# A transformer layer on one core: a new beginning, both first halves first, and the causal mask of four groups added by VectorE

## The reference, cut to what matters

```python
x = x + attention(layernorm(x))          # x: 2 sequences x 1024 tokens x 128
x = x + moe(layernorm(x))

def attention(x):                        # 16 heads of 8, causal
    q, k, v = x @ Wq.T, x @ Wk.T, x @ Wv.T         # per head
    q, k = rope(layernorm_head(q)), rope(layernorm_head(k))
    s = where(tril, q @ k.T / sqrt(8), -inf)
    return (softmax(s) @ v) @ Wo.T + bo

def moe(x):                              # 16 experts of 64, 2 per token, one shared of 128
    p = softmax(x @ gate_w.T)            # best 2 of 4 groups of experts, then best 2 experts
    y = sum_e combine[:, e] * (silu(x @ We1 + be1) * (x @ We3 + be3) @ We2 + be2)
    return y + silu(x @ ws1 + bs1) * (x @ ws3 + bs3) @ ws2 + bs2
```

## Time and profile before

| | |
|---|---|
| median of 3 runs | 455.01 us (453.49 to 484.75) |
| the profiled execution | 456.76 us, of it a span of 454.9 us from the first to the last instruction |
| busy share of the span | PE 84%, DVE 68%, ACT 59%, POOL 44% |
| mean granted TensorE clock | 0.910 |

### The profile page before, as it was taken

One profiled execution on the slowest core, in us unless ns is written; L12 is line 12 of the kernel. 1 busy time (PEld: TensorE's weight loads), 2 busy tenths in 40 slices (PEclk: granted clock), 3 DMA queues, 4 the chain that ended last, 5 costly groups with the idle time before them and its releaser, 6 DMA issues.

```text
span 454.9 us, 6876 instructions
## 1 busy us (share of the span) xinstructions
PE 382.1 (84%) x2295; PEld 138.7 (30%) x2295; DVE 309.4 (68%) x622; ACT 269.6 (59%) x395; POOL 198.7 (44%) x294
## 2 busy tenths in 40 slices
PE   3542898779599898999997999998988999979786
PEld 2221233132133242223243332222423322434332
DVE  4676978795827897558355899757878761439543
ACT  2524048337659844185877943684585799865460
POOL 1304966964693424144141454632222332268441
PEclk9865659868979998699999999999999999997899
DMA  6966023000400035000050044000000001540271
GB/s 146 181 116 138 1 57 86 0 2 1 118 22 4 1 79 110 1 1 2 1 141 3 1 98 90 2 1 0 3 0 2 1 3 46 112 78 0 55 134 46
DMA packets 26036, 21.48 MB, mean 47 GB/s; under 512 B 8817, under 2 KB 21778, under 8 KB 25938
## 3 DMA queue, kind: packets, MB, share of 16 engines
q1 hardware_dynamic: 24610, 19.99, 20.3%
q10 hardware_dynamic: 1392, 1.05, 1.1%
HBM read 13.43 MB, written 1.18 MB: 32 GB/s over the span
## 4 chain that ended last, share of the span: by engine, by line
PE 48%; DVE 16%; ACT 10%; DMA 8%; issue 7%; POOL 7%; SPq 2%; ACTq 1%; POOLq 0%; DVEq 0%
PE psum L809 11%; PE psum L791 7%; PE psum L844 6%; PE psum L855 6%; PE psum L767 6%; DMA comb_b<-combine_scratch 5%; DVE mx_full L1199 5%; ACT probs L917 4%; PE psum L732 3%; PE psum L761 3%; DVE mx_diag L1199 3%; PE psum L741 1%; ACT sq L934 1%; PE psum L859 1%; DMA xs<-in_x 1%
## 5 line engine op out<-in xcount | busy, mean ns | idle before, releaser
L917 ACT ACTIVATE probs<-psum 128x1024 f32<-128x1024 f32 x144 | 140.6, 1027 | 24.1 <-PE psum L791 21.7
L1199 DVE TENSOR_REDUCE mx_diag<-psum 128x4 f32<-128x512 f32 (+2 forms) x96 | 97.3, 1041 | 41.2 <-PE psum L767 40.8
L1199 DVE TENSOR_REDUCE mx_full<-psum 128x2 f32<-128x1024 f32 x64 | 75.8, 1218 | 24.3 <-PE psum L767 24.1
L1111 POOL TENSOR_SCALAR_AFFINE_SELECT probs<-probs 128x256 f32<-128x256 f32 (+1 forms) x112 | 47.6, 442 | 90.4 <-ACT probs L917 87.9
L809 PE MATMUL psum<-probs,v_ones 128*9 128x512 f32 (+3 forms) x768 | 79.8, 505 | 6.9 <-POOL probs L1111 6.6
L844 PE MATMUL psum<-x2T,w 128*128 128x512 f32 x144 | 77.1, 639 | 5.8 <-ACT mv L954 2.7
L1121 POOL TENSOR_TENSOR mh<-mh,mv 128x512 f32<-128x512 f32 x36 | 45.6, 1270 | 76.6 <-DVE mv L1271 76.6
L767 PE MATMUL psum<-k_st,q_st 62*128 62x512 bf16 (+3 forms) x384 | 61.7, 356 | 3.1 <-DVE mx_full L1199 2.9
L791 PE MATMUL psum<-q_st,k_st 64*128 64x512 bf16 (+3 forms) x384 | 54.3, 333 | 8.7 <-ACT probs L917 6.4
L855 PE MATMUL psum<-mh,w 128*128 128x512 f32 x72 | 42.6, 693 | 6.0 <-POOL mh L610 3.4
L1271 DVE SCALAR_TENSOR_TENSOR mv<-psum,b,mv 128x512 f32<-128x512 f32 x36 | 26.4, 745 | 23.6 <-ACT mh L966 23.5
(11 more groups left out here) (150 smaller groups left out, 393.3 us busy)
## 6 DMA issues: line engine op xcount, KB each, us to landing
comb_b<-combine_scratch SPq DMA_DIRECT2D x8, 1024.0 KB, 10.0
q_st<-parts SPq DMA_DIRECT2D x24, 128.0 KB, 2.5
k_st<-parts SPq DMA_DIRECT2D x18, 128.0 KB, 2.5
w<-in_We SPq DMA_DIRECT2D x3, 512.0 KB
k_st<-in_c_pad SPq DMA_DIRECT2D x2, 512.0 KB, 8.1
out<-xs SPq DMA_DIRECT2D x4, 256.0 KB, 2.3
xs<-in_x SPq DMA_DIRECT2D x3, 256.0 KB, 10.2
k_st<-parts ACTq DMA_DIRECT2D x6, 128.0 KB, 4.1
```

What stands on the lines that cost most here:

```text
L917: act.activation(probs[:, n % P_RING, :, :], wpair("scores", (s, i)), ACT.Exp, scale=SCALE).then_inc(exp_done, 1)
L1111: last = pool.affine_select(out=v, in_=v, compare_op=ALU.is_ge, fill=0.0, base=0, pattern=[[0, v.shape[1]], [1, P]], channel_multiplier=-1)
L1199: dve.tensor_reduce(dst[:, a % 2, qt, :, pairs[0]:pairs[0] + nm], w, AX.X, ALU.max, negate=True).then_inc(max_free, 1)
```

## The change

1. **Order of the chunks.** Chunk x becomes half `x // 2` of sequence `x % 2`: both first halves, then both second halves.
2. **The layernorm before attention is folded away.** The raw x is transposed. The weights are centred by one more product (`wcenter`: with I - 1/128). q and k need no factor of the token, since each head is normalised again (the epsilon is scaled by the token's variance: `eps_x`); v is multiplied by the token's reciprocal root as ACT copies it (`values`). `norm` splits into `stats` and `norm`; `norm_apply` and `xn` go.
3. **Chunk 0's preparation is cut by tiles** and spread over ACT (`square`), DVE (`products`, `headsum0`, straight from PSUM), POOL (`join`); the factor of the head comes last (`rope_q`, then `rope_k`, so that `qT` starts before k is ready). Its lowest part of k is made by DVE.
4. **The reciprocal roots** take 8 operations on DVE (a Newton step, then a step of higher order), not 10; on POOL 12 of other kinds, not 15. The stages of POOL are cut finer (seven for a chunk).
5. **Loads.** Inputs are packed on the host; SP issues 10 loads, not 39. `w_attn` is issued by ACT behind chunk 0's x. The padding rows are set by memsets: `q_st` by DVE, `k_st` by POOL, each half of `k_st` on its own. `stack` waits for each of the three parts by itself.
6. **`mneg` of groups 0 to 3** is done by DVE (`mneg_dve`).
7. **Groups 4 to 7** (now the first half of sequence 1): no mask matmuls. DVE adds the mask and takes the maximum in one `tensor_tensor_reduce` for each head's rows.
8. **The planner** has other lengths, windows and `PV_LAG`, and `NUDGES`, which shift the urgency of single stages.

The diff, cut to its core (the numbers of `NUDGES`, the packing on the host and renamings are left out):

```diff
+def seq_of(x):
+    return x % B
+def half_of(x):
+    return x // B
+def keys_of(x):
+    return [y for y in range(x + 1) if seq_of(y) == seq_of(x)]
...
-PREP_WINDOWS = ((-282.3, -241.5), (-192.9, -118.6), (269.8, 447.0), (500.9, 602.6))
-EPILOGUE_WINDOWS = ((-268.0, -266.3), (-631.0, -532.6), (262.1, 401.0), (76.9, 130.6))
-MOE_WINDOWS = ((52.4, 357.9), (166.5, 310.2), (303.6, 553.6), (401.9, 560.1))
-PV_LAG = 152.8
+PREP_WINDOWS = ((-728.2, -501.8), (-276.2, -260.9), (325.2, 359.2), (740.3, 741.2))
+EPILOGUE_WINDOWS = ((-259.4, -227.3), (-714.1, -661.4), (253.0, 450.8), (-388.2, 27.1))
+MOE_WINDOWS = ((52.1, 369.6), (329.2, 365.2), (381.8, 511.7), (442.6, 536.5))
+PV_LAG = 126.2
+SPLIT_ON_DVE = NG
+MASKED_BY_DVE = range(4,8)
+ROPE_OF = ((),) + (("rstd_seed", "rstd_step", "rope_scale", "rope_cos", "rope_sin", "rope_add", "rope_join"),) * 3
...
+            if part == 0:
+                if which == 0 and x >= 2:
+                    engine.wait_ge(work_full, turned(*LAST_SCORES[NG * (x - 1) - 1]))
+                elif which == 0:
+                    engine.wait_ge(q_blank, 1)
+                else:
+                    engine.wait_ge(k_blank, b + 1)
+                engine.wait_ge(part_hi, 2 * x + which + 1)
+            elif part == 1:
+                engine.wait_ge(part_mid, 2 * x + which + 1)
+            elif (x, which) == (0, 1):
+                engine.wait_ge(first_low, 1)
+            else:
+                engine.wait_ge(parts_lo, 2 * x + which + (x == 0))
+            for t in [t for t, p in enumerate(terms) if p == part]:
+                engine.dma_start(dst[t::HD], parts[:, which, part, :]).then_inc(done, 16)
...
+            sp.dma_start(mats[:, :, :], c_mats).then_inc(ld_attn, 16)
+            sp.dma_start(rowb[:, :], vectors.partition_broadcast(P)).then_inc(ld_tabs, 16)
+            sp.dma_start(tabs[:, :], c_tabs).then_inc(ld_tabs, 16)
+            sp.dma_start(xs[:, 1, :, :], x_v[1]).then_inc(ld_x[1], 16)
+            sp.dma_start(gate_raw, gate_w).then_inc(ld_gate, 16)
+            sp.dma_start(experts[:, :], w_moe).then_inc(ld_moe, 16)
+            sp.dma_start(b2[:, :], b_moe).then_inc(ld_moe, 16)
...
+            def whole():
+                w = fill("wcenter", 0)
+                pe.wait_ge(work_read_act, frees("act", turned("weights", 0)))
+                pe.matmul(w[:, 0:3 * P], whole_mean, w_whole, start=True, stop=True).then_inc(work_full, 1)
...
+                masked_here = what == "diag" and a not in MASKED_BY_DVE
+                if masked_here:
                     for par in range(2):
                         v = w[:, par, 0:nm * keys].rearrange("p (m k) -> p m k", m=nm)[:, :, keys - P:keys]
                         pe.matmul(v, ident_bf[:, :], causal_bf[:, :].unsqueeze(1).broadcast_to([P, nm, P]),
...
             act.dma_start(xs[:, 0, :, :], x_v[0]).then_inc(ld_x[0], 16)
+            act.dma_start(w_raw[:, :, :], w_attn).then_inc(ld_attn, 16)
...
+            def first_products(t):
+                dve.wait_ge(squared, t + 1)
+                both = wbank("qkv0", t)[:, 0:2 * P]
+                cos = g_cos[:, 0, t, :, :, :].rearrange("p w r d -> p (w r d)")
+                dve.tensor_tensor(first_cos[:, t, :, :], both.rearrange("p (n m) -> p n m", m=H // 2),
+                                  cos.unsqueeze(2).broadcast_to([P, 4 * HD, H // 2]), ALU.mult)
...
+            def first_rope(w):
+                dve.wait_ge(joined, TPC)
+                r = hrstd[:, :].rearrange("p (t n m) -> p t n m", t=TPC, m=H // 2)
+                for par in range(2):
+                    s = roped[:, :, w, par, :, :]
+                    last = dve.tensor_tensor(s, s, r[:, :, 2 * w + par, :].unsqueeze(2).broadcast_to(
+                        [P, TPC, HD, H // 2]), ALU.mult)
+                link(last)
+                for par in range(2):
+                    s = roped[:, :, w, par, :, :]
+                    last = dve.tensor_tensor(s, s, g_add[:, 0, :, w, par, :].unsqueeze(3).broadcast_to(
+                        [P, TPC, HD, H // 2]), ALU.add)
+                last.then_inc(first_roped, 1)
...
-                dve.tensor_reduce(dst[:, a % 2, qt, :, pairs[0]:pairs[0] + nm], w, AX.X, ALU.max, negate=True).then_inc(max_free, 1)
+                if what == "full" or a not in MASKED_BY_DVE:
+                    last = dve.tensor_reduce(dst[:, a % 2, qt, :, pairs[0]:pairs[0] + nm], w, AX.X, ALU.max, negate=True)
+                else:
+                    for par in range(2):
+                        for i, m in enumerate(pairs):
+                            last = dve.tensor_tensor_reduce(
+                                w[:, par, i, :], w[:, par, i, :], causal[:, CH - keys:], -1.0, -MASKED, ALU.add,
+                                ALU.min, dst[:, a % 2, qt, par, m:m + 1])
+                last.then_inc(max_free, 1)
```

729 lines of the change are left out of this document (465 added, 264 removed).

## The result

The changed kernel takes **469.89 us** (median of 4 runs, 468.79 to 470.59) against 457.2 for the kernel before on the same chip: ratio **1.030, interval 1.021 to 1.039**, slower by some 13 us. One of before's four executions, 484.75 us, fell in a slower state that this kernel shows now and then; it is in the median 457.2 and not in the ratio, which is 469.8 over 456.0. The forecast was 436 us, 4% faster. Its profiled execution spans 466.8 us, before's 454.9.

A forecast was written before the change was run, and what follows sets the result against it. PE was taken as the bound from first scores to the last attention copy (90% busy). Scores at 46 plus 389.5 gave 435.5, with 1.86 around it 437.4, less 1.75 for the median: 436 us, main range 431 to 442.

The forecast's parts named there:

- Part 3: PE after the first scores: 346.5 us of busy work, times before's factor 1.124, takes 389.5 us.
- Part 2: First max matmul to first scores: 13 us once queue waits go; scores at 46, 20.8 us earlier.
- Part 1: Chunk 0's preparation chain: first max matmul at 33, 10.5 us earlier, between 5 and 12.
- Part 4: DVE's fused maxima in groups 4 to 7: 3 to 6.5 us more in all, hidden, 0 on the path.
- Part 5: The rest, including ACT's applies, SP's loads, POOL's finer stages and chunk order: nothing beyond what other parts count.
- rival of a shorter end, The end shrinks too: Tail after attention: chunk 2's experts stop delaying chunk 3's gate and routing, 9 us less, 427 us; chance 22%.
- too little work early: Chunk 0's short groups run out before chunk 1's keys come, a PE gap of 14 us, 450 us; chance 14%.
- slower: Groups 4 to 7: the fused operation makes two passes, DVE bounds them, 30 us more, 466 us; chance 5%.
- Held queues: ACT's or POOL's order again delays the first maxima, so 13 us of early scores come back, 449 us; chance 10%.

The follow-up runs named there:

- e5: The changed kernel with every mask on PE and windows, lag and nudges searched afresh: 451.21 us, ratio 0.986 against before.
- e1: The changed kernel, order untouched, with the masks of groups 4 to 7 back on PE: 467.56 us, ratio 1.024 against before.
- e8: e5 with its queue order unchanged and the fused masks in groups 4 to 7 as in the changed kernel: 458.88 us, ratio 1.009 against before.
- e2: The kernel before with only the fused maxima in groups 4 to 7: 453.99 us, ratio 0.994 against before.
- e3: The new beginning with before's sequence of chunks, windows and lag, no nudges, all masks on PE: 492.45 us, ratio 1.077 against before.
- e4: e3 with new numbers in windows, lag and nudges, so the same operations in another queue order: 457.48 us, ratio 1.001 against before.
- e10: The changed kernel with every mask on PE, order searched again after two planner numbers were set to the profile's: 467.82 us, ratio 1.022 against before.
- e7: The changed kernel, operation for operation, with other windows and nudges: 471.10 us, ratio 1.029 against before.
- e17: e2 with each chunk's combine-weight load split in two pieces, a quarter of the bytes first: 448.13 us, ratio 0.986 against before.
- e13: e1 without each chunk's combine-weight load, experts weighted with numbers loaded once from x (not the reference): 449.34 us, ratio 0.984 against before.
- e16: e13 with first-half groups' maxima also cut to a quarter of the keys (not the reference): 444.73 us, ratio 0.971 against before.
- e9: The changed kernel's operations, order searched again after two planner numbers were set to the profile's: 463.66 us, ratio 1.013 against before.

## Why the prediction was wrong

The step that failed is **Part 3**: "345.2 + 9 - 7.7 = 346.5; times 1.124 = 389.5". It took the PE share of before's time after the first scores as a property of the kernel and kept it when the order of all queues changed. From the first scores on the new kernel has 292.09 + 58.55 = 350.6 us of PE work and takes 414.5 for it, a factor of 1.182. Of the 31.3 us by which the span misses 435.5, 6.3 are scores that came later than 46, 4.7 are 4.1 us of work more than counted, times 1.124, and 350.6 x 0.058 = 20.3 are the factor.

Behind it stands an assumption about **Part 2**: that 20.8 us of earlier scores are won unless the work is missing. The first scores are not what the end hangs on. Before had PE busy 20.09 of its 23.20 us ahead of them; the lead in busy time was 3.4 us, and e5 with its scores at 72.2 is the fastest of the orders.

Point by point:
- **Part 1** was right: first max at 35.3, inside the bounds of 31.5 to 38.5, by steps of which two were mis-sized (weights at 7.58, not 4.8; qkv 2.8, not 5.0), so the number owes something to luck. The terms written down for the start of qkv add up to 8.5, not 9.4, and leave out the transposes of x, which stand on the chain at 9.01 with 0.85. PE's queue, with chunk 1's qkv in front of chunk 0's transposes, had no term. Of the 2.5 us of locks one operation shows some 0.5: L1405, 0.78 at 18.25 and 0.29 at 41.51. The blank of q_st was 4096 columns and 3.47 us, where I had 2048 and 1.9; DVE's statistics start at 6.28 for it, still ahead of the weights.
- **Part 2**'s mechanism was right, its size 14.4 where I had 20.8: the first max comes 2.3 us later than 33, and from there to the first scores it takes 17.0, not 13, since the max units wait for DVE in between and, at a granted clock of 0.50, share PE with the preparation of chunk 2.
- **Part 4**: a fused operation costs one pass (0.726 at 512 columns, forecast at most 0.75) and an accumulator read of 0.142. DVE's busy time grew by 6.2 from e1 to after and by 6.0 from e5 to e8; forecast were 3 to 6.5. Its cover was named as "71% use", a mean over the old stretch. In e2 it held; in e8 it was gone, and the price was 7.7; in after's own order, e1 over after, 2.3, with overlapping intervals.
- **Part 5** gave the sequence of chunks and the nudges nothing, since they change "no amount of work". They decide which waits are covered, and with the same operations that is worth 35 us (e3 to e4), 16.6 (e10 to e5) and 12.2, or 9 by the ratios (e7 to e8). The wait for the combine weights was in the rows I quoted, with 3.33 us of POOL; it stood in the rival of a shorter end and not in the sum; the landing behind it takes 12.1, and a wait on the chain costs more through the clock.
- The rival **too little work early** named the early stretch and the sign of the loss but stopped at 450; the rival **slower**, 466, came near the time by the wrong mechanism (two passes, where the trace shows one), and that is luck. **Held queues** did not occur on ACT or POOL. **The end shrinks too** did not come: it grew by 3.

The 13 us from before to after, as far as the cuts show them: the combine loads cost e1 18.2 and before 10.8, a difference of 7.4; DVE's first-half maxima 5.4 and 1.5, a difference of 3.9; the fused operation some 2.3. Together 13.6. By the ratios the three are some 7.8, 1.3 and 2.9, together 12. They were not measured in one design, each difference carries an error of some 3 us, and that they come so near to the 13 is in part chance. If they hold, the earlier start is worth about nothing. e17 shows that the waits cost something with all of the computation in place; e13 to e16 leave part of it out. Why the planner can't tell these orders apart isn't settled: two of its numbers were off from the profile, and e9 and e10 show that mending them isn't enough.

## What to carry to other kernels

Compare how much bound-engine work is done at given times, not when a milestone is passed: 14 us of earlier scores were 3 us of work. A cover is a place and not a mean, so an operation "hidden at 71% use" has to be looked up where the new order puts it. When a queue order is made anew, count the long fixed latencies that stand on the chain before and after; shortening one of them (e17) was worth 4 to 6 us, about what the new beginning gave in its best order (e5, 6.3 under before).
